# A transformer block pair on one core: store buffers of the first projections moved into tensors that are used later, and one fill of the attention's operands moved behind a load

## What is computed

```python
# layer 0, attention: 16 heads of 8, causal
x = x + _L0_attn_ref(_layernorm(x), Wq, bq, Wk, bk, Wv, bv, Wo, bo)
    q, k, v = x @ Wq + bq, x @ Wk + bk, x @ Wv + bv
    scores = einsum('bhqd,bhkd->bhqk', q, k) / sqrt(8)
    scores = where(causal, scores, -10000.0)
    out = einsum('bhqk,bhkd->bhqd', softmax(scores), v) @ Wo + bo
x = x + _L0_ffn_ref(_layernorm(x), ...)     # experts, then layer 1: attention with top-k, experts
```

## Time and profile before

| | |
|---|---|
| median of 3 runs | 3257.57 us (3254.95 to 3259.0) |
| the profiled execution | 3257.62 us, its span 3255.9 us |
| busy share of the span | TensorE 79%, VectorE 82%, ScalarE 74%, GpSimd 62% |
| first projections | up to 88.4 us |
| first attention, pieces ahead | 88.4 to 126.2 us |
| first attention, slot 0 of item 0 | 130.8 us |
| DMA, mean over the span | 26 GB/s |

### The profile page before, as it was taken

How to read it: one execution, slowest core, us unless ns; L and a number is a source line. 1 busy time by engine, 2 the same in 40 slices (tenths; PEclk the granted TensorE clock), 3 DMA queues, 4 the chain that set the end, 5 groups by cost and what they waited for, 6 DMA issues and landing times. The chain is left out here.

```text
span 3255.9 us, 73507 instructions
## 1 busy us (share of the span) xinstructions
PE 2563.6 (79%) x23705; PEld 1428.2 (44%) x23705; DVE 2682.6 (82%) x8599; ACT 2396.8 (74%) x4003; POOL 2014.2 (62%) x4527
## 2 busy tenths in 40 slices
PE   3799999769657777777777777775777777779999
PEld 2233333234424454444444544453454444445444
DVE  6788888344759999999999999998999999947444
ACT  3266666524249999999999999997999999933221
POOL 4034333420359999999999999997899999920000
PEclk8699999979866778777778777777777778779999
DMA  5321211001320101101100110110100110010000
GB/s 164 91 56 47 58 48 43 13 26 30 76 65 2 18 2 18 19 5 16 19 11 10 18 17 4 18 18 2 18 14 7 19 17 4 2 34 4 7 7 10
DMA packets 115269, 85.94 MB, mean 26 GB/s; under 512 B 58153, under 2 KB 97339, under 8 KB 114875
## 3 DMA queue, kind: packets, MB, share of 16 engines
q1 hardware_dynamic: 106683, 76.38, 10.7%
q0 software_dynamic: 8192, 4.79, 1.0%
HBM read 54.25 MB, written 19.40 MB: 23 GB/s over the span
## 5 line engine op out<-in xcount | busy, mean ns | idle before, releaser
L1412 POOL TENSOR_TENSOR a_near<-a_side,a_z 128x1024 int32<-128x1024 int32 x512 | 968.7, 1892 | 42.7
L1308 PE MATMUL a_ST<-a_qs,a_ks 75*128 75x128 bf16 x4096 | 655.0, 249 | 394.2 <-DVE a_mask L1545 215.7
L1508 DVE MAX8 a_cand<-a_near 128x8 f32<-128x256 f32 x2048 | 810.6, 414 | 0.0
L1308 PEld LDWEIGHTS a_ST<-a_qs,a_ks 75*128 75x128 bf16 x4096 | 457.6, 113 | 561.7 <-DVE a_mask L1545 340.2
L1552 DVE TENSOR_SCALAR_CACHE_REDUCE a_z<-a_S,a_thr 128x1024 f32<-128x1024 f32 x512 | 649.7, 1269 | 14.5 <-POOL a_thr L1388 8.4
L1332 ACT ACTIVATE a_signs<-a_z,a_tiny 128x1024 bf16<-128x1024 f32 x512 | 588.7, 1150 | 75.1 <-DVE a_z L1552 71.7
L1325 ACT ACTIVATE a_signs<-a_S,search 128x1024 bf16<-128x1024 f32 x512 | 571.0, 1115 | 5.3 <-PE a_S L1263 5.2
L1347 ACT ACTIVATE a_eT<-a_ST 128x1024 f32<-128x1024 f32 x512 | 518.9, 1014 | 16.3 <-PE a_ST L1309 16.0
L996 ACT ACTIVATE a_eT<-a_ST 128x512 f32<-128x512 f32 (+3 forms) x768 | 329.2, 489 | 216.1 <-PE a_ST L981 155.0
L1263 PE MATMUL a_S<-a_ks,a_qs 72*128 72x512 bf16 x1024 | 394.5, 475 | 81.7 <-DVE a_z L1552 75.7
L1100 DVE TENSOR_REDUCE a_mx<-a_S 128x1 f32<-128x512 f32 (+3 forms) x768 | 380.9, 547 | 82.4 <-PE a_S L968 66.8
(11 more groups left out here) (365 smaller groups left out, 4401.4 us busy)
## 6 DMA issues: line engine op xcount, KB each, us to landing
a_qs<-q_parts SPq DMA_DIRECT2D x176, 64.0 KB
a_ks<-k_parts SPq DMA_DIRECT2D x176, 64.0 KB
a_qs<-a_flip SPq DMA_DIRECT2D x512, 0.8 KB
q_parts<-p_qp SPq DMA_DIRECT2D x48, 128.0 KB, 2.0
k_parts<-p_kp SPq DMA_DIRECT2D x48, 128.0 KB, 2.2
a_qs<-q_parts SPq DMA_DIRECT2D x64, 96.0 KB
a_ks<-k_parts SPq DMA_DIRECT2D x64, 96.0 KB
f_w<-L_ffn_W SPq DMA_DIRECT2D x16, 256.0 KB, 2.9
```

The costliest lines, as they stand in the source:

```text
L1308: pe.matmul(ST[:, block_of], ks[:, base(hl) + kb * P:base(hl) + (kb + 1) * P], qs[:, tile(hl):tile(hl) + P], start=True, stop=False)
L1412: pool.tensor_tensor(near[:, hl % NEARS, :].bitcast(I32), side[:, one].bitcast(I32).broadcast_to([P, SEQ]), z[:, hl % H, :].bitcast(I32), ...
L1508: mm = dve.max(found[:, 8 * g:8 * g + 8], near[:, h2 % NEARS, g * SW:(g + 1) * SW])
```

## The change

The store buffers qp and kp have no memory of their own any more: qp is a view of ctxT (the first 1536 bfloat16 columns of each of its four rows of 1024 float32), kp the same of `packed`. vst and the semaphores `stored` move out of `project0` to the scope around both stages. With that, nothing that attention writes at its start is still being read by a store; the four waits for all stores leave the end of the projections, and stand instead in attention's SP list ahead of the first `step` and in GpSimd's list ahead of its first `step`. The third fill, which stood ahead of those waits at the end of the projections, is issued in attention, behind the load of pass 1.

```diff
+HELD, STORES = 4, 16 * (2 * SPLIT + 1)
@@ build
-                project0(nc, k, ln0)
                 ctxT = front.enter_context(nc.sbuf_tensor("ctxT", [P, 4, SEQ], F32))
+                k.vst = [front.enter_context(nc.sbuf_tensor(f"p0_vst{c}", [P, CT, D], F32)) for c in range(HELD)]
+                k.stored = [front.enter_context(nc.semaphore(f"p0_stored{c}")) for c in range(HELD)]
+                project0(nc, k, ln0, ctxT, packed)
                 attention0(nc, k, ctxT, packed)
@@ project0
-        qp, kp = four(sb, "qp", [D, SPLIT, CW], BF16), four(sb, "kp", [D, SPLIT, CW], BF16)
-        vst = four(sb, "vst", [P, CT, D])
+        spare = lambda a: a.bitcast(BF16)[:, 0:SPLIT * CW].rearrange("p (s t) -> p s t", s=SPLIT)
+        qp, kp = [spare(ctxT[:, c, :]) for c in range(HELD)], [spare(packed[:, c * SEQ:(c + 1) * SEQ]) for c in range(HELD)]
+        vst, stored = k.vst, k.stored
...
             for n in range(CB + 1, NCH):
                 store(n)
-            fill_pass0(sp, k, 2)
-            for held in range(HELD):
-                sp.wait_ge(stored[held], STORES * NCH // HELD)
@@ attention0, SP
             load_pass0(sp, k, 1)
+            fill_pass0(sp, k, 2)
             sp.wait_ge(kq_in[0], 16 * DMAS_Q)
             sp.wait_ge(k.blank_s[2], 64)
             load_pass0(sp, k, 2)
             store_max(0)
             fill_pass0(sp, k, 3)
             sp.wait_ge(k.blank_s[3], 64)
+            for c in range(HELD):
+                sp.wait_ge(k.stored[c], STORES * NCH // HELD)
             for it in range(ITERS):
                 step(it)
@@ attention0, GpSimd
             copy_v(0, 0)
             copy_v(0, 1)
+            for c in range(HELD):
+                pool.wait_ge(k.stored[c], STORES * NCH // HELD)
             for it in range(ITERS):
                 step(it)
```

More of the change, by code:

```diff
@@ L254, in setup, with project0 @@
     nc.all_engine_barrier()
-def project0(nc, k, pre):
+def project0(nc, k, pre, ctxT, packed):
     mean, rstd = pre
-    HELD = 4
-    STORES = 16 * (2 * SPLIT + 1)
     with ExitStack() as ctx:
@@ L273, in pair @@
             return [make(f"{name}{c}", *a) for c in range(2)]
-        def four(make, name, *a):
-            return [make(f"{name}{c}", *a) for c in range(HELD)]
         xn, xT = pair(sb, "xn", [P, CT, D]), pair(sb, "xT", [D, CW])
@@ L286, in project0 @@
         qres_s, cast_s, qlast_s, ksplit = (sem(x) for x in ("qres", "cast", "qlast", "ksplit"))
-        stored = four(sem, "stored")
         block = ctx.enter_context(nc.Block())
```

## The result

| | before | after |
|---|---|---|
| median, 14 runs each | 3256.95 us | 3262.7 us |
| lowest to highest | 3253.99 to 3259.29 | 3259.23 to 3266.3 |
| span of the profiled execution | 3255.9 us | 3264.5 us |
| first instruction of VectorE in attention | 88.52 us | 84.34 us |
| slot 0 of item 0 | 130.8 us | 135.8 us |

The ratio is 1.0018, with a 95% interval of 1.001 to 1.0026: the changed kernel is slower by 5.75 us between the medians, a difference clear of the noise, just within the 0.2% that the prediction called the same. The profiled execution, 3266.3 us, is the slowest of the fourteen, so its span alone would make the change look 3 us worse than it is.

What follows compares the result with a forecast made beforehand. The queue of a few loaded DMA engines bounds slot 0: moving the fill costs it 4.6 us plus 2.9 of emptiness, less 4.0 from an earlier start, so 3.3 us later: 3260.9 us, range 3254.2 to 3264.0.

Steps and rivals of the forecast that it cites:

- Start of attention set by the fills' issue, not by the waits: End of projections: removing the waits for stores is worth nothing, moving the fill 3.2 us; attention starts at 85.2.
- Slot 0 held by the queue of a few loaded DMA engines: First attention: slot 0 waits for that queue to drain; about six idle us of TensorE and VectorE are slack before it.
- SP waits for fill 2, until 111.1: Between passes 1 and 2: SP held until 111.1 us by fill 2, where pass 2 was issued at 99.95 before.
- Fill 2's sharing and own part, 4.6 us: Loaded DMA queue between the passes: fill 2 costs 2.9 us by sharing and 1.7 us of its own, together 4.6.
- Two passes with lead and landing, 38.1 us: Loaded queue before slot 0: each pass 17.5 us of work, 0.5 us lead to first byte, 2.3 us final landing.
- Emptiness, 2.9 us: Between passes 1 and 2: the queue stands empty for 2.4 us of fill 2's landing and 0.5 us of lead.
- Sharing of fill 3 with pass 2, 2.9 us: End of pass 2, before slot 0: fill 3, issued behind the maxima, takes nearly 2.9 us from pass 2.
- One to one to the end: From slot 0 to the kernel's end: the 3.3 us delay is carried in full, 3257.62 to 3260.9 us.
- Rival 1: Start of attention: its gain is carried through, slot 0 at 127.6, total 3254.4 us; chance 0.13.
- rival 2: Between the passes: fill lands regardless of the queue, SP resumes near 104, +0.4, total 3258.0 us; chance 0.15.
- rival 4: End of the kernel: later waits swallow 3 us, nothing changes, total 3257.6 us; chance 0.05.
- Rival 3: Between the passes: fill 2's own part is a full fill's time, SP released past 114.5, total 3264.5 us; chance 0.09.

Runs made afterwards that it cites:

- e1: Changed kernel with the third fill (fill 2) put back at the end of the projections: 3256.33 us, ratio 0.9999.
- e3: Kernel before with only fill 2 moved behind pass 1, buffers and waits for stores left in place: 3265.42 us, ratio 1.0025.
- e4: Changed kernel with fills 2 and 3 made by eight GpSimd memsets in place of eight DMAs: 3248.88 us, ratio 0.9979.
- e10: Changed kernel with fill 2 issued between the two halves of pass 1 instead of after it: 3260.76 us, ratio 1.0006.
- e5: Changed kernel with fill 3 moved up behind fill 2, so both are issued behind pass 1: 3264.39 us, ratio 1.0019.
- e11: Changed kernel with fills 2 and 3 made by GpSimd memsets, run once more: 3249.28 us, ratio 0.9977.
- e9: Kernel before with only fills 2 and 3 made by GpSimd memsets, old buffers and waits for stores kept: 3253.31 us, ratio 0.9987.
- e7: Changed kernel with all four fills made by GpSimd, fills 0 and 1 in the projections: 3250.06 us, ratio 0.9976.
- e8: Changed kernel measured once more, unaltered, as a yardstick: 3265.21 us, ratio 1.0029.
- e6: Kernel before with SP waiting for item 0's maxima to land before it issues fill 3: 3255.34 us, ratio 0.9992.
- e2: Changed kernel with fill 2 as attention's first DMAs, ahead of the load of v: 3258.76 us, ratio 1.0005.

## Why the prediction was right, and where it was short

The sign, the mechanism and the range held; the shift was 5.75 us where the sum said 3.3. From pass 1's first issue to slot 0 the sum has 48.3 us (85.8 to 134.1) and the trace 51.1. The term that was mis-sized is the cost of fill 2 to the loaded queue: 4.6 in the sum, 7.4 in the runs.

- **Start of attention set by the fills' issue, not by the waits.** Right: e1 puts the fill back and gains nothing, e3 moves it alone and finds 1.5 us of wait. The start came at 84.3, against 85.2, since the stores were through 0.7 us sooner in this profile.
- **Slot 0 held by the queue of a few loaded DMA engines.** Right: the start moved 4.2 us forward and slot 0 moved back; with the queue relieved (e4) slot 0 came 9.9 us before that of the kernel before, almost to where VectorE ends. That few engines are at work is read from the share; no run changed the shapes of the passes.
- **SP waits for fill 2, until 111.1.** It was 111.4. This close agreement hides an error: pass 1 had begun 1.1 us sooner than assumed, and from its first issue to SP's release it took 26.7 us, against 25.3 in the sum.
- **Fill 2's sharing and own part, 4.6 us: too small by 2.8.** The 1.7 us of own part came from taking the drained queue (128.5) and fill 3's landing (130.2) each as a release less 2.3 or 2.4 us. e10 and e5 both give 7.4 for a fill that SP waits for. Which of the two parts was taken too small, the sharing or the own part, no run separates.
- **Two passes with lead and landing, 38.1 us: too large by 1.0.** e4 has 37.1 (the 37.3 and 37.5 of e11 and e9 agree; e7 has 38.1).
- **Emptiness, 2.9 us: too small by about 0.8.** The sum had 2.4 us for the landing and 0.5 from issue to first byte. The trace has them the other way round: SP is released at most 1.2 us after the last movement (110.25:110.50 still has a share of 0.07), and the share is still 0.00 in 113:114, 2.6 us after the issue at 111.40. Together that is 3.5 us, and e10 gives 3.7 us back (4.6 against e8). That the hole exists is shown; that it costs its length fits e10 and isn't proved by it alone.
- **Sharing of fill 3 with pass 2, 2.9 us.** Right: 41.8 - 38.9 in e6. In the changed kernel the sum had 2.7 for it; there it was not measured.
- **The terms together:** 2.8 + 0.8 + 0.2 - 1.0 = 2.8, the 51.1 against 48.3. Pass 1 began 1.1 us sooner, so slot 0 came 1.7 us behind the 134.1: 5.0 us later than before, not 3.3. These are differences between single profiles, good to about 1 us, so that they close to the tenth is luck.
- **One to one to the end.** Nearly: +5.0 at slot 0, +6.1 at item 10, +5.75 in the medians. In e3 it was +7.6, +8.6 and +9.1; in e6 -4.0, -3.6 and -3.1. In e4 it was -9.9, -9.1 and -7.5: the medians give 2.4 us less than slot 0, while the span of that one profiled execution shrank by 10.6 (3255.9 to 3245.3), so the gap is within the spread of single executions.
- **The Trainium skill.** The Trainium skill's rule that a DMA uses the largest number of engines, up to 16, that divides its slowest dimension (DMA: Bandwidth & Descriptors, section on why a DMA increments its semaphore by 16) agrees with a share of 0.19 of 16 while a pass is alone; no run changed those dimensions. The Trainium skill's fit of 2.0 us plus the bytes over 436 GB/s (the same page, section on the anatomy of a DMA; made for GpSimd's path) doesn't carry over to SP's DMAs behind a loaded queue: a 256 KB DMA of fill 2 landed after 14.3 us, where an estimate by the fit gives 2.6.
- **Rivals.** Rival 1 (the gain is carried) is refuted by slot 0 at 135.8 and again by e2, rival 2 (the fill lands without regard to the queue) by the 14.3 us, rival 4 (nothing changes at the end) by the 5.75 us. Rival 3 (slower) had a premise that came true, a fill's part larger than was summed, but by its own sign it fell: SP's wait ended at 111.4, not after 114.3. The result lies between the forecast and rival 3.

## What to carry to other kernels

Before moving a transfer, ask in which queue it will stand and which wait in the issuing list is for it: a fill that is free ahead of an idle stretch costs 9.3 us when it stands between two long loads of which the second waits for it (51.1 against 41.8 from pass 1 to slot 0; 4.4 of them came back here by the earlier start of pass 1). An earlier start only pays if what ends the next idle stretch also comes earlier; read the releaser of that stretch first. And an idle engine may be the better place for work that a DMA does with constants: eight memsets of 1.8 us on GpSimd turned a loss of 5.75 us into a gain of 7.5.

## What the runs showed of the hardware that I had not expected

When the queue had run empty, the first bytes of pass 2 moved 2.6 us or a little more after SP issued it (111.40 to the first share in 114:115); for pass 3 in the kernel before, issued at 132.56, the share is back in 134:135, that is after 1.4 to 2.4 us (share 0.24 in the window of 134:135 shown with the result). The other two kernels of the changed order show less than 2.6: in e3, issued at 113.84, the share is back in 115.0:115.5, in e8, issued at 112.42, in 113.5:114.0 or, after another empty window, in 114.5:115.0. All are above the 0.5 us that I had put in. What sets the length, and whether the times of the two kinds of record are offset against each other, is open.

A fill of 1 MB costs the loaded queue very different amounts by where it stands: 1.8 us ahead of pass 1 (41.8 - 37.1 - 2.9), 2.9 us behind the maxima (e6), 7.4 us between two passes of which the second waits for it (e10, e5), and nothing when GpSimd writes it.
